# Depthwise stage: ACT issues the stores of its own copies, and POOL prepares the stage's constants and zero rows inside the pointwise stage

## The reference, cut to what matters

```
x = gn(x)                                             # group norm over 32 groups
qkv = einsum('bchw,oc->bohw', x, qkv_w)               # pointwise: 192 -> 576 channels
qkv = conv3d(qkv, qkv_dw_w, groups=576, pad=1)        # depthwise 3x3: 576 channels, 4 images of 128x128
gate = relu(einsum(x, gate_w1) + b1); sigmoid(einsum(gate, gate_w2) + b2)   # its mean is used later
q, k, v = split(qkv)      # 192 channels each; then attention scores, a second convolution, the output
```

## Time and profile before

| | us |
|---|---|
| median of 3 runs | 7432.79 |
| lowest and highest run | 7431.01, 7443.61 |
| the profiled execution, its own time | 7438.61 |
| its span | 7435.9 |
| pointwise stage in the trace, first transfer to the barrier | 164.28 to 1274.36 |
| depthwise stage | 1274.36 to 2490.27 |

### The profile page before, as it was taken

How to read it: one execution, slowest core, us unless ns; L and a number is a source line. 1 busy time by engine, 2 the same in 40 slices (tenths; PEclk the granted TensorE clock), 3 DMA queues, 4 the chain that set the end, 5 groups by cost and what they waited for, 6 DMA issues and landing times. The chain is left out here.

```text
span 7435.9 us, 82986 instructions
## 1 busy us (share of the span) xinstructions
PE 5760.8 (77%) x25278; PEld 2354.1 (32%) x25278; DVE 5662.4 (76%) x5546; ACT 2748.5 (37%) x3703; POOL 341.1 (5%) x539
## 2 busy tenths in 40 slices
PE   0999997799899566455565777699768879985888
PEld 0333332333333465233332222232222223222222
DVE  6333332799999777888885666599979978997998
ACT  0222221111111466111110000055479974556998
POOL 0110100000000000122220000000000000000000
PEclk9999998899999787777777788787779988787999
DMA  7556554999999997899997999754456644445665
GB/s 292 174 177 198 182 190 152 221 270 274 270 275 277 235 230 179 209 247 255 248 249 181 267 270 267 189 186 183 164 198 230 231 164 170 183 178 182 231 230 181
DMA packets 1209065, 1615.58 MB, mean 217 GB/s; under 512 B 87604, under 2 KB 907509, under 8 KB 1195509
## 3 DMA queue, kind: packets, MB, share of 16 engines
q1 hardware_dynamic: 1067125, 1419.06, 65.6%
q10 hardware_dynamic: 115200, 100.71, 5.1%
q0 software_dynamic: 26624, 94.40, 5.1%
HBM read 1006.55 MB, written 607.33 MB: 217 GB/s over the span
## 5 line engine op out<-in xcount | busy, mean ns | idle before, releaser
L501 PE MATMUL dw_p<-dw_it,dw_tt 128*128 128x512 f32 x2304 | 1027.1, 607 | 177.0 <-DMA dw_it<-u 176.3
L541 DVE SCALAR_TENSOR_TENSOR dw_vo<-dw_vi,dw_wv,dw_vo 128x2048 f32<-128x2048 f32 x384 | 903.1, 2352 | 13.6
L836 PE MATMUL bc_p<-bc_z,bc_wc 128*32 128x256 f32 x9216 | 572.8, 414 | 399.4 <-DVE bc_z L875 399.4
L289 PE MATMUL pw_p<-pw_xh,pw_wlo 128*112 128x512 f32 x1536 | 693.2, 601 | 184.4 <-POOL pw_xh L263 184.4
L875 DVE STREAM_TRANSPOSE bc_z<-bc_xp 128x1536 f32<-128x1536 f32 x256 | 711.8, 2850 | 154.1 <-DMA bc_xp<-d 153.7
L1084 PE MATMUL ap_p<-ap_vt,ap_pw 96*96 96x512 f32 x1024 | 584.3, 736 | 186.5 <-DMA ap_xt<-in_x 184.7
L501 PEld LDWEIGHTS dw_p<-dw_it,dw_tt 128*128 128x128 f32 x2304 | 441.7, 193 | 762.5 <-issue 745.4
L516 ACT ACTIVATE dw_ot<-dw_p 128x512 f32<-128x512 f32 x384 | 206.7, 608 | 997.3 <-DMA d<-dw_ot 703.6
L344 DVE COPY pw_ut<-pw_p 112x512 f32<-112x512 f32 x384 | 247.3, 685 | 379.5 <-PE pw_p L295 377.5
L836 PEld LDWEIGHTS bc_p<-bc_z,bc_wc 128*32 128x32 f32 x9216 | 323.8, 119 | 648.5 <-issue 487.2
L814 ACT ACTIVATE bc_xt<-bc_p 128x256 f32<-128x256 f32 x384 | 147.4, 384 | 874.7 <-PE bc_p L836 874.7
(11 more groups left out here) (310 smaller groups left out, 9845.4 us busy)
## 6 DMA issues: line engine op xcount, KB each, us to landing
u<-pw_ut SPq DMA_DIRECT2D x64, 2240.0 KB, 12.6
dw_it<-u SPq DMA_DIRECT2D x192, 512.0 KB, 7.2
d<-dw_ot SPq DMA_DIRECT2D x192, 512.0 KB, 7.3
gr_qk<-d SPq DMA_DIRECT2D x128, 768.0 KB, 9.0
bc_xp<-d SPq DMA_DIRECT2D x256, 288.0 KB, 12.0
bc_xp<-d POOLq DMA_DIRECT2D x256, 288.0 KB, 9.9
gs_xt<-in_x SPq DMA_DIRECT2D x24, 2048.0 KB, 7.2
d<-dw_vo SPq DMA_DIRECT2D x96, 512.0 KB, 7.8
```

What stands on the lines that cost most here:

```text
L289: mm(pt[m % NBANK][e][:, :], wlo[:, wm], xh[:, h, 2 * e, cols], start=True, stop=False, skip_group_check=True)
L501: mm = nc.tensor.matmul(po[c][:, :].rearrange("p (b w) -> p b w", b=B), tt[:, h, 3 * c + dx, 0:H], it[:, h, B * c:B * (c + 1), dx:dx + W], ...
L541: nc.vector.scalar_tensor_tensor(vo[:, h], src, w, vo[:, h], ALU.mult, ALU.add).then_inc(tapped, 1)
L836: mm = nc.tensor.matmul(po[q % NBANK][32 * c4:32 * c4 + 32, :, :], wc[:, c, dx, :, :].rearrange("p j r -> p (j r)"), z[:, h, c, :, dx:dx + ...
```

## The change

The constants `tw`, `wv` and `mask` become buffers that outlive a stage (`depthwise_consts`) and are made in the pointwise stage by POOL, together with the zero rows of `d`. POOL does this after its first two tiles (`norm(0)`), with transfers of its own queue; the clearing of `zero` stands ahead of these tiles. The depthwise stage has neither the loads of constants nor the zero rows nor the mask any more. In its loop, the four stores of `ot` are taken from SP's turn and issued by ACT right behind the eight copies they store. The semaphore `stored` that ACT waits on is now started by ACT.

```
 def pointwise(...)
+        tw, wv, mask = consts
+        zero = st.sb("zero", [128, ROW // 128])
...
         def _(pool):
             pool.wait_ge(weights, NWL)
-            with pool.Fori(0, NJ) as j:
+            nc.gpsimd.memset(zero[:, :], 0.0).then_inc(masked, 1)
+
+            def norm(j):
                 for h in range(2):
...
                     last.then_inc(normed, 1)
+            norm(0)
+            pool.wait_ge(masked, 1)
+            for p in range(3):
+                pool.dma_start(tw[p:128:3, :, :].rearrange("p m i -> p (m i)"),
+                               bass.AP(turned_w.tensor, p * 18 * C, [[0, len(range(p, 128, 3))], [1, 18 * C]])).then_inc(early, 16)
+            taps = dww[2 * C:C3].rearrange("(g p) a d y x -> p (a g) (d y x)", p=64)[:, :, 9:18]
+            for p in (0, 64):
+                pool.dma_start(wv[p:p + 64, :, :], taps).then_inc(early, 16)
+            for b in range(B):
+                for at in (0, PAD_IMG - ROW):
+                    pool.dma_start(d[b, at:at + ROW].rearrange("(p n) -> p n", p=128), zero[:, :]).then_inc(early, 16)
+            nc.gpsimd.memset(mask[:, :], 1.0).then_inc(masked, 1)
+            for k, (sign, base) in enumerate(((1, 2 - H), (-1, H))):
+                pool.wait_ge(masked, k + 2)
+                nc.gpsimd.affine_select(out=mask[:, :], in_=mask[:, :], compare_op=ALU.is_ge, fill=0.0, base=base,
+                                        pattern=[[sign, H + 1]], channel_multiplier=sign).then_inc(masked, 1)
+            with pool.Fori(1, NJ) as j:
+                norm(j)
+            pool.wait_ge(early, 16 * (5 + 2 * B))
+            pool.wait_ge(masked, 4)
...
 def depthwise(...)
-        def store(sp, n, h):
-            sp.wait_ge(by_act, GC * (n + 2))
+        def store(act, n, h):
+            act.wait_ge(by_act, GC * (n + 2))
+            own_wait(act, passed)
             for b in range(B):
                 img = d[b, ROW:ROW + C3 * HW].rearrange("(c h w) -> h c w", h=H, w=W)
-                sp.dma_start(img[:, bass.ds(n * GC, GC), :], ot[:, h, :, b * W:(b + 1) * W]).then_inc(stored[h], 16)
+                act.dma_start(img[:, bass.ds(n * GC, GC), :], ot[:, h, :, b * W:(b + 1) * W]).then_inc(stored[h], 16)
...
         def _(sp):
-            (loads of tw and wv, wait for zero, eight stores of zero rows, wait for their landing)
             sp.wait_ge(padded, 1)
             for h in range(2):
-                sp.sem_inc(stored[h], 1)
                 sp.sem_inc(v_stored[h], 1)
                 load_v(sp, 0, h)
                 load(sp, h, h)
...
                     store_v(sp, b, k)
-                    store(sp, n, h)
...
         def _(act):
             act.sem_inc(by_act, GC)
+            for h in range(2):
+                act.sem_inc(stored[h], 1)
...
                         nc.scalar.activation(ot[:, h, c, :], po[c][:, :], ACT.Copy).then_inc(by_act, 1)
+                    store(act, n, h)
...
         def _(dve):
-            nc.vector.memset(zero[:, :], 0.0).then_inc(cleared, 1)
-            dve.wait_ge(wl, 48)
-            dve.wait_ge(masked, 3)
             for h in range(2):
                 build(nc.vector, h, h)
-            dve.wait_ge(v_weights, 32)
```

More of the change, by code:

```diff
@@ L156, in by_row, with depthwise_consts, pointwise @@
     return ap.rearrange("p (r w) -> p r w", w=W)
-def pointwise(nc, x, stat0, w1t, gate_b1, w2t, gate_b2, u, gate_sums):
+def depthwise_consts(nc, ctx):
+    return [ctx.enter_context(nc.sbuf_tensor(f"keep_{name}", shape, F))
+            for name, shape in (("tw", [128, 6 * C, 3]), ("wv", [128, C // 64, 9]), ("mask", [128, H + 1]))]
+def pointwise(nc, x, stat0, w1t, gate_b1, w2t, gate_b2, u, gate_sums, dww, turned_w, consts, d):
     M, NM = 112, 6
@@ L184, in pointwise @@
         pz = st.ps("pz", [128, SUB])
+        tw, wv, mask = consts
+        zero = st.sb("zero", [128, ROW // 128])
+        early, masked = st.sem("early"), st.sem("masked")
         weights, spread, gsum_stored, passed = map(st.sem, ("weights", "spread", "gsum_stored", "passed"))
@@ L349, in _, with depthwise @@
                                             accum_out=gs[:, bass.ds(n, 1)]).then_inc(by_dve, 1)
-def depthwise(nc, u, dww, turned_w, d):
+def depthwise(nc, u, consts, d):
     GC = 8
@@ L367, in depthwise @@
     S = NV * NR
-    NZD = 2 * B
     assert B * S == NG and NR % 2 == 0
+    tw, wv, mask = consts
     uv = u.rearrange("c b (h w) -> h (c b) w", w=W)
     with Stage(nc, "dw") as st:
[L372 to L375, removed]
         it = st.sb("it", [128, 2, GC * B, W + 2])
@@ L381, in depthwise @@
         po = [st.ps(f"p{c}", [128, B * W]) for c in range(GC)]
-        wl, cleared, masked, built, zeros_stored, padded = map(
-            st.sem, ("wl", "cleared", "masked", "built", "zeros_stored", "padded"))
-        v_weights, passed = st.sem("v_weights"), st.sem("passed")
+        built, padded, passed = map(st.sem, ("built", "padded", "passed"))
         loaded = [st.sem(f"loaded{h}") for h in range(2)]
@@ L484, in _ @@
             last.then_inc(padded, 1)
[L485 to L489, removed]
         @block.tensor
@@ L1826, in build @@
     group_stats(nc, x, stat0)
-    pointwise(nc, x, stat0, io["w1t"], io["gate_b1"], io["gate_w2t"], io["gate_b2"], u, gate_sums)
-    depthwise(nc, u, io["qkv_dw_w"], io["turned_w"], d)
+    with ExitStack() as kept:
+        consts = depthwise_consts(nc, kept)
+        pointwise(nc, x, stat0, io["w1t"], io["gate_b1"], io["gate_w2t"], io["gate_b2"], u, gate_sums,
+                  io["qkv_dw_w"], io["turned_w"], consts, d)
+        depthwise(nc, u, consts, d)
     gram_scores(nc, d, io["temperature"], attn_d)
```

## The result

The changed kernel takes 7372.15 us (median of 4 runs, 7365.53 to 7389.65), the kernel before 7435.32 (4 runs, 7431.01 to 7443.61): a ratio of 0.991, with a 95% interval of 0.9894 to 0.9925. Forecast were 7371.1 us and a gain of 61.7; the medians lie 63.2 apart. The interval allows a gain from 56 to 79 us, so that the two agree to 1.5 us is partly luck.

A forecast was written before the change was run, and what follows sets the result against it. DVE was taken to bound the depthwise loop at 23.59 us a turn, leaving the stage's start and end to gain: -54.7 + 0.6 - 7.6 = -61.7 us, a median of 7371.1 us; own range 7363 to 7386, stated 7364 to 7388.

The forecast's parts named there:

- Start, 54.7 us: Depthwise stage start: without constants and zero rows SP's first `vi` issue moves from 1329.58 to 1274.9, gaining 54.7 us.
- the wait of 10.8 us: End of the depthwise loop's first turn: DVE's only wait for PE after its first tap, forecast to stay.
- POOL, 0.6 us: Pointwise stage: clearing `zero` ahead of the first tile costs 0.6 us; POOL's transfers and mask hide in idle time.
- the upper bound of 46.7 us from SP's row: Pointwise stage: POOL's thirteen transfers cost 46.7 us if they hold POOL as long as SP, under 60.7 us of cover.
- Stores on ACT, 0.0 us in the loop: Depthwise loop: ACT issuing the `ot` stores is worth 0.0 us, covered by DVE's 23.59 us turn against PE's 22.56.
- End, 7.6 us: Depthwise stage end: last `ot` stores go out before the last tap, the end waits for `vo` alone; gain 7.6 us.
- parts 2 and 4: POOL's pointwise work, costing 0.6 us, and the depthwise stage's end, gaining 6.4 to 8.9 us; their bounds enter the range.
- A: Depthwise loop: two queues disturb each other and transfers become the bound; 7450 full, 7404 mild; chance 0.06 each.
- the 254 below which the change would have lost: Depthwise loop: transfer rate of 254 GB/s, 1.6 us more per turn, from which the whole change is a loss.
- B: Pointwise stage: POOL's 43-row transfers hold POOL 93 us, making the tile 33 us late once; 7404; chance 0.04.
- the slow carrier: 43-partition loads are carried by one transfer engine at 29 GB/s, filling it for 41 us also in the pointwise stage.
- C: Depthwise loop: ACT's 703.6 us of waiting was the bound, so turns shorten towards 21.3 us; 105 us more, 7266; chance 0.01.

## Why the prediction was right, step by step

1. *Start, 54.7 us.* Right in size and place: first issue 1274.75 for 1274.9, first tap 1284.17 for 1284.1, builds hidden, clock of 0.50 and the wait of 10.8 us unchanged. The account of it was coarse: 38 us hung on the shape of one load, which the run with pieces of 32 gets back without any move.
2. *POOL, 0.6 us.* 0.58 measured for the clearing. In the whole it can't be seen: POOL's first instruction came 1.1 us earlier in this execution (179.65 for 180.76), and the depthwise stage starts 0.2 us earlier than before. The 7.2 us of issue by POOL's own row were 7.40; the upper bound of 46.7 us from SP's row was the price of SP's queue and says nothing of POOL's.
3. *Stores on ACT, 0.0 us in the loop.* Right: 23.59 and 23.58 us a turn, and the two runs with one part each have the same loop. ACT's four issues took 10.54 us, not SP's 8.89, still with 8 us of the turn to spare. Its cover, DVE, is what decides: with a shorter DVE turn the same stores are worth about 99 us (112.2 less 13.6, what leaving out the ninth tap gains with two queues and with one).
4. *End, 7.6 us.* 14.91 less 7.26 is 7.65.

In the trace the first tap comes 54.6 us earlier, the stretch from there to the last tap is as long as before to 0.1 us, and the end is 7.65 shorter: 62.2 in all, where 61.7 were forecast. One step of the working doesn't come out: the range of 7363 to 7386 is said to follow from the bounds of parts 2 and 4 and the spread, but these give about 7368 to 7384. The measured median lies in both.

Of the rivals, A had its direction wrong: two queues carried 303 GB/s where one stopped at 272, so the 254 below which the change would have lost was never neared. Half of its premise was right: one queue was at its end. The share of 1.13 was no proof that the engines could carry no more, since the same rate cost 0.98 with ACT's stores. B rested on the slow carrier, which POOL's queue doesn't have. C was refuted by ACT's stores alone.

## What to carry to other kernels

A long wait of one engine (703.6 us) is worth nothing until somebody who bounds the loop waits for that engine; the ends of a stage, where nobody computes, are worth their full length. Before moving a slow load, look at its shape: a plateau of 29 GB/s, where other stretches reach 290 to 400, was the sign here, and pieces of 32 rows instead of 43 gave 38 of 55 us. To learn how near a second resource is to the bound, shorten the first one and see where the turn stops.

## What the runs showed of the hardware that I had not expected

- Two issuing queues carried 303 GB/s in a loop in which one was stuck at 272, with the same transfers. At 271 GB/s the share of the transfer engines' time fell from 1.13 to 0.98 with the stores of `ot` on ACT's queue.
- Loads of 43 rows crawled at 29 GB/s on SP's queue and held what was queued behind them; the same loads on POOL's queue had landed 8.6 us after the first issue.
- POOL's builds of 7.4 us took 5.9 us of each turn from DVE, and nearly all of it in one instruction: the median tap stayed at 2352 ns, the longest took 8394.
